# A state-space block with a gated feed-forward part on one core: two GpSimd chains of four operations per chunk become one chain over eight columns

## The reference

```python
x = x + attn(layernorm(x))     # attn: in_proj -> causal conv (4 taps) -> silu -> dt, B, C
                               # h[t] = exp(delta*A)*h[t-1] + delta*B*x  (16 states x 512 channels)
                               # y = sum_n h*C + D*x ; out_proj(y * silu(z))
x = x + ffn(layernorm(x))      # shared expert relu(x Ws1)^2 Ws2, plus top-2 of 8 experts weighted by
                               # trunc(softmax weight), which is 0 unless one weight is 1
```

## Time and profile before

| | us |
|---|---|
| median of 3 runs | 1577.25 (1576.58 to 1578.4) |
| the profiled execution's own time | 1574.1 |
| its span in the trace | 1572.0 |
| busy in the span: DVE, PE, POOL, ACT | 1474.5, 1443.9, 1411.7, 1258.6 |
| mean granted TensorE clock | 0.994 of full |

### The profile page before, as it was taken

One profiled execution on the slowest core, in us unless ns is written; L12 is line 12 of the kernel. 1 busy time (PEld: TensorE's weight loads), 2 busy tenths in 40 slices (PEclk: granted clock), 3 DMA queues, 4 the chain that ended last, 5 costly groups with the idle time before them and its releaser, 6 DMA issues.

```text
span 1572.0 us, 39373 instructions
## 1 busy us (share of the span) xinstructions
PE 1443.9 (92%) x15160; PEld 1119.7 (71%) x15160; DVE 1474.5 (94%) x1773; ACT 1258.6 (80%) x2100; POOL 1411.7 (90%) x1248
## 2 busy tenths in 40 slices
PE   8788999999999999999999999999999999998876
PEld 5666777776777777777776777777777677776765
DVE  6999999999999999999999999999999999998884
ACT  7887887887888888787888888788788888787651
POOL 2899998999999999998999999899998999899893
PEclk9999999999999999999999999999999999999998
DMA  5103031040402204031130402204031130402201
GB/s 154 65 3 135 2 105 60 13 152 3 153 12 69 95 3 162 2 122 42 22 143 3 162 1 77 89 3 162 3 131 33 42 110 3 149 1 86 79 15 42
DMA packets 78512, 106.46 MB, mean 68 GB/s; under 512 B 42289, under 2 KB 67761, under 8 KB 70130
## 3 DMA queue, kind: packets, MB, share of 16 engines
q1 hardware_dynamic: 78322, 103.92, 20.6%
HBM read 86.10 MB, written 17.30 MB: 66 GB/s over the span
## 4 chain that ended last, share of the span: by engine, by line
DVE 29%; ACT 19%; PE 19%; issue 16%; POOL 11%; DMA 2%; SPq 2%; DVEq 1%; ACTq 0%; POOLq 0%
DVE hs L941 26%; POOL hs L1229 9%; PE BX L236 8%; ACT da L605 8%; PE Y L296 3%; SPq L1358 2%; DMA cb<-c_scratch 2%; PE Y L260 2%; ACT xc L672 1%; PE PB L346 1%; ACT u L710 1%; ACT xp L640 1%; ACT x2n L742 1%; ACT u L708 1%; DVE Y L972 1%
## 5 line engine op out<-in xcount | busy, mean ns | idle before, releaser
L1229 POOL TENSOR_TENSOR hs<-hs,cb 128x1024 f32<-128x1024 f32 x512 | 1211.8, 2368 | 67.1 <-DVE hs L941 45.2
L941 DVE TENSOR_TENSOR_SCAN hs<-da,BX 128x512 f32<-128x512 f32 x1024 | 1165.5, 1201 | 61.0 <-PE BX L236 51.5
L605 ACT ACTIVATE da<-delta,a_neg 128x511 f32<-128x511 f32 (+1 forms) x1024 | 663.5, 711 | 25.1 <-DVE hs L941 24.8
L260 PEld LDWEIGHTS Y<-ident,hs 128*128 128x128 f32 x4096 | 464.4, 141 | 96.2 <-issue 61.5
L260 PE MATMUL Y<-ident,hs 128*128 128x128 f32 x4096 | 511.9, 273 | 11.1 <-POOL hs L1229 11.0
L236 PE MATMUL BX<-bd,uT 32*128 32x128 f32 x8192 | 302.7, 284 | 97.3 <-DVE hs L941 93.0
L236 PEld LDWEIGHTS BX<-bd,uT 32*128 32x128 f32 x8192 | 253.6, 187 | 157.9 <-DVE hs L941 155.4
L296 PE MATMUL Y<-xnT,w_in 128*128 128x512 f32 x240 | 118.1, 615 | 0.9 <-ACT xnT L621 0.9
L640 ACT ACTIVATE xp<-Y 128x512 f32<-128x512 f32 x60 | 35.9, 599 | 100.3 <-PE Y L296 99.7
L321 PE MATMUL PA<-w_in,xnT 128*128 128x512 f32 x240 | 114.5, 599 | 0.0
L972 DVE SCALAR_TENSOR_TENSOR Y<-xp,w_conv,Y 128x512 f32<-128x512 f32 x120 | 88.8, 740 | 2.3 <-ACT Y L642 0.7
(11 more groups left out here) (184 smaller groups left out, 1493.7 us busy)
## 6 DMA issues: line engine op xcount, KB each, us to landing
cb<-c_scratch SPq DMA_DIRECT2D x64, 1024.0 KB, 4.8
x<-in_x SPq DMA_DIRECT2D x16, 512.0 KB, 3.9
x_scratch<-x2T SPq DMA_DIRECT2D x16, 512.0 KB, 6.8
xt<-in_x SPq DMA_DIRECT2D x15, 512.0 KB, 4.9
bd<-bt SPq DMA_DIRECT2D x480, 1.0 KB
out<-x SPq DMA_DIRECT2D x15, 512.0 KB, 3.1
w_in<-in_in_wT SPq DMA_DIRECT2D x1, 1024.0 KB, 8.3
c_scratch<-dbc SPq DMA_DIRECT2D x64, 8.0 KB, 1.5
```

The lines of the kernel that those rows point to most:

```text
L260: mm = e.matmul(Y[(G * c + g) % 2][:, t * P:(t + 1) * P], hs[:, k % HR, q, t * P:(t + 1) * P], ident[:, :], is_transpose=True, start=False ...
L605: e.activation(da[:, k % DR, q, h:], delta[:, g, h:], ACT.Exp, scale=a_neg[:, g, n:n + 1]).then_inc(s_da, 1)
L941: e.tensor_tensor_scan(hs[:, k % HR, q, :], da[:, k % DR, q, :], BX[:, :].rearrange("p (t n) -> p n t", n=RT)[:, n % RT, :], float(c % HV) ...
L1229: e.tensor_tensor(hs[:, k % HR, :, :], hs[:, k % HR, :, :], cb[:, Q * p:Q * p + Q, :], ALU.mult).then_inc(s_hc, 1)
```

## The change

The chain of the second norm of chunk c - 1 and the chain of the input norm of chunk c + 3 become one chain over eight columns, at s == 21, for the chunks c = 1 to 12 of the loop (`BOTH`). The tiles `mv`, `ve`, `rstd`, `neg` and `shift` become eight columns wide; their first half serves the input norm, their second half the second norm. In these chunks the chain counts on the semaphores of the input norm, so those who wait for the second norm's result wait for `s_sh` (`shifted2`). It waits for both aggregations. In chunk 0 the input norm's chain, still four columns, moves from s == 25 to s == 21. In chunks 13 to 15 `pool_rstd2` stays as it was. The count waits of the last chunk are renumbered to fit.

```diff
@@ -96,19 +96,18 @@
-        mhalf = sb("mhalf", [P, TB])
-        minus = sb("minus", [P, TB])
-        epsv = sb("epsv", [P, TB])
+        mhalf = sb("mhalf", [P, 2 * TB])
+        minus = sb("minus", [P, 2 * TB])
+        epsv = sb("epsv", [P, 2 * TB])
...
-        mv = sb("mv", [P, TB, 2])
...
-        shift = sb("shift", [P, TB])
+
+        mv_b, ve_b, rstd_b, neg_b, shift_b = (sb("mv", [P, 2 * TB, 2]), sb("ve", [P, 2 * TB]), sb("rstd", [P, 2 * TB]),
+                                              sb("neg", [P, 2 * TB]), sb("shift", [P, 2 * TB]))
+        mv, ve, rstd, neg, shift = (mv_b[:, 0:TB, :], ve_b[:, 0:TB], rstd_b[:, 0:TB], neg_b[:, 0:TB], shift_b[:, 0:TB])
@@ -129,11 +128,8 @@
-        mv2 = sb("mv2", [P, TB, 2])
...
-        shift2 = sb("shift2", [P, TB])
+        mv2, ve2, rstd2, neg2, shift2 = (mv_b[:, TB:2 * TB, :], ve_b[:, TB:2 * TB], rstd_b[:, TB:2 * TB],
+                                         neg_b[:, TB:2 * TB], shift_b[:, TB:2 * TB])
@@ -170,6 +166,12 @@
+        BOTH = (1, NQ - 4)
+
+        def shifted2(c):
+            return (s_sh, c + 5) if c + 1 <= BOTH[1] else (s_sh2, c + 1 - BOTH[1])
@@ -732,7 +734,7 @@
         def act_norm2(e, c):
-            e.wait_ge(s_sh2, c + 1)
+            e.wait_ge(*shifted2(c))
@@ -996,7 +998,8 @@
         def dve_aggr2(e, c):
             e.wait_ge(s_st2, TB * (c + 1))
-            e.wait_ge(s_sh2, c)
+            if c:
+                e.wait_ge(*shifted2(c - 1))
@@ -1251,24 +1254,30 @@
         def pool_rstd(e, c):
             e.wait_ge(s_mv, TB * (c + 1))
             e.wait_ge(s_xn, c)
-            e.tensor_tensor(ve[:, :], mv[:, :, 1], epsv[:, :], ALU.add).then_inc(s_ve, 1)
-            e.tensor_tensor(neg[:, :], mv[:, :, 0], minus[:, :], ALU.mult).then_inc(s_neg, 1)
+            n = TB
+            if BOTH[0] <= c - 3 <= BOTH[1]:
+                n = 2 * TB
+                e.wait_ge(s_mv2, TB * (c - 3))
+                e.wait_ge(s_xn2, c - 4)
+            e.tensor_tensor(ve_b[:, 0:n], mv_b[:, 0:n, 1], epsv[:, 0:n], ALU.add).then_inc(s_ve, 1)
+            e.tensor_tensor(neg_b[:, 0:n], mv_b[:, 0:n, 0], minus[:, 0:n], ALU.mult).then_inc(s_neg, 1)
             e.wait_ge(s_ve, c + 1)
-            e.tensor_tensor(rstd[:, :], ve[:, :], mhalf[:, :], ALU.pow).then_inc(s_rs, 1)
+            e.tensor_tensor(rstd_b[:, 0:n], ve_b[:, 0:n], mhalf[:, 0:n], ALU.pow).then_inc(s_rs, 1)
             e.wait_ge(s_neg, c + 1)
             e.wait_ge(s_rs, c + 1)
-            e.tensor_tensor(shift[:, :], neg[:, :], rstd[:, :], ALU.mult).then_inc(s_sh, 1)
+            e.tensor_tensor(shift_b[:, 0:n], neg_b[:, 0:n], rstd_b[:, 0:n], ALU.mult).then_inc(s_sh, 1)
@@ -1309,11 +1318,11 @@
-                    if s == 21 and on(c - 1):
+                    if s == 21 and c > BOTH[1]:
                         pool_rstd2(e, c - 1)
                     if s == 30 and on(c - 1):
                         pool_gap(e, c - 1)
-                    if s == 25 and on(c + 3):
+                    if s == 21 and on(c + 3):
                         pool_rstd(e, c + 3)
```

More of the change, by code:

```diff
@@ L106, in mamba_moe @@
         st = sb("st", [P, TB, 6])
-        mv = sb("mv", [P, TB, 2])
-        ve = sb("ve", [P, TB])
-        rstd = sb("rstd", [P, TB])
-        neg = sb("neg", [P, TB])
-        shift = sb("shift", [P, TB])
+        mv_b, ve_b, rstd_b, neg_b, shift_b = (sb("mv", [P, 2 * TB, 2]), sb("ve", [P, 2 * TB]), sb("rstd", [P, 2 * TB]),
+                                              sb("neg", [P, 2 * TB]), sb("shift", [P, 2 * TB]))
+        mv, ve, rstd, neg, shift = (mv_b[:, 0:TB, :], ve_b[:, 0:TB], rstd_b[:, 0:TB], neg_b[:, 0:TB], shift_b[:, 0:TB])
         xnT = [sb(f"xnT{i}", [P, KD, CH]) for i in range(2)]
@@ L131, in mamba_moe @@
         st2 = sb("st2", [P, TB, 6])
-        mv2 = sb("mv2", [P, TB, 2])
-        ve2 = sb("ve2", [P, TB])
-        rstd2 = sb("rstd2", [P, TB])
-        neg2 = sb("neg2", [P, TB])
-        shift2 = sb("shift2", [P, TB])
+        mv2, ve2, rstd2, neg2, shift2 = (mv_b[:, TB:2 * TB, :], ve_b[:, TB:2 * TB], rstd_b[:, TB:2 * TB],
+                                         neg_b[:, TB:2 * TB], shift_b[:, TB:2 * TB])
         x2n = sb("x2n", [P, TB, DM])
@@ L907, in scalar @@
             for h in range(2):
-                e.wait_ge(s_sh2, NQ + h)
+                e.wait_ge(s_sh2, NQ - BOTH[1] + h)
                 for t in (2 * h, 2 * h + 1):
@@ L1193, in vector @@
                 e.wait_ge(s_st2, TB * (NQ - 1) + 2 * (h + 1))
-                e.wait_ge(s_sh2, NQ - 1)
+                e.wait_ge(*shifted2(NQ - 2))
                 for t in (2 * h, 2 * h + 1):
@@ L1264, in pool_rstd2 @@
             e.wait_ge(s_xn2, c)
[L1265 to L1271, removed]
+            n = c + 1 - BOTH[1]
+            e.tensor_tensor(ve2, mv2[:, :, 1], epsv[:, 0:TB], ALU.add).then_inc(s_ve2, 1)
+            e.tensor_tensor(neg2, mv2[:, :, 0], minus[:, 0:TB], ALU.mult).then_inc(s_neg2, 1)
+            e.wait_ge(s_ve2, n)
+            e.tensor_tensor(rstd2, ve2, mhalf[:, 0:TB], ALU.pow).then_inc(s_rs2, 1)
+            e.wait_ge(s_neg2, n)
+            e.wait_ge(s_rs2, n)
+            e.tensor_tensor(shift2, neg2, rstd2, ALU.mult).then_inc(s_sh2, 1)
         def pool_gap(e, c):
@@ L1325, in gpsimd @@
                 e.tensor_tensor(neg2[:, part], mv2[:, part, 0], minus[:, part], ALU.mult).then_inc(s_neg2, 1)
-                e.wait_ge(s_ve2, NQ + h)
+                e.wait_ge(s_ve2, NQ - BOTH[1] + h)
                 e.tensor_tensor(rstd2[:, part], ve2[:, part], mhalf[:, part], ALU.pow).then_inc(s_rs2, 1)
-                e.wait_ge(s_neg2, NQ + h)
-                e.wait_ge(s_rs2, NQ + h)
+                e.wait_ge(s_neg2, NQ - BOTH[1] + h)
+                e.wait_ge(s_rs2, NQ - BOTH[1] + h)
                 e.tensor_tensor(shift2[:, part], neg2[:, part], rstd2[:, part], ALU.mult).then_inc(s_sh2, 1)
```

## The result

| | before | after |
|---|---|---|
| median, timed side by side, 20 runs each, us | 1575.96 (1572.54 to 1581.81) | 1572.35 (1568.34 to 1579.87) |
| ratio, 95% interval | | 0.9978 (0.9969 to 0.9987) |
| the same, in a second session of 11 runs and 29 of before | 1575.99 | 1573.14, ratio 0.9982 (0.9973 to 0.9991) |
| profiled execution, its span | 1574.1, 1572.0 | 1571.58, 1569.8 |

The change makes the kernel faster by 0.2%. The profiled execution is close to what the sum said (1571.5, and a span of 1569.4). That it comes so close is luck: a second profiled execution of the same kernel took 1568.82. The two hardly differ up to the first scan of chunk 15 (1445.66 and 1445.67 us from the start), and from there to the end, where TensorE's clock fell at other places in each, it is 124.1 us in the first, 121.4 in the second and 124.3 before.

A forecast was written before the change was run, and what follows sets the result against it. The prediction took a DVE and PE ring with a 5.85 us beat as the bound. 3.5 us won less 0.9 lost gave 2.6 off the 1577.25 median: 1574.6, range 1572.6 to 1578.4.

The forecast's parts named there:

- the sum: Whole kernel: 3.5 us won less 0.9 lost, 2.6 us off, for a profiled execution of 1571.5 and span of 1569.4.
- The bound: DVE and PE form a ring, four scans and the refill of `BX`, 5.85 us per pair of steps; POOL matters only where late.
- The price of the power: POOL's chain at step 21: power costs 156 ns a column, 1638 ns for eight, so the chain grows 0.63 us.
- The rival by which the price is one per instruction: POOL's chain does not grow with eight columns, nothing is lost at step 26, all 3.5 us come: 1573.7; chance 0.1.
- Step 30: Even chunks 2 to 12: POOL's product of step 27 comes earlier, beat falls from 6.37 to 5.85, 0.52 us won six times.
- The rival with PE's own order in its place: PE's order at step 29 holds step 30 in even chunks; only 0.34 won against 0.9 lost: 1577.8; chance 0.12.
- Step 26: Even chunks: the longer merged chain makes `BX` 0.08 to 0.21 us late, taken as 0.15 six times, 0.9 us lost; odd chunks nothing.
- The rest, at nothing: ACT's second norm, the wait for both aggregations, step 25's u, DMA and wider constants were all said to cost nothing.
- Chunk 0: Moving its four-column chain from step 25 to 21 returns 0.34 us at step 30, where the beat was 6.19.
- The slower case: POOL's power at eight columns costs more than 156 ns a column; break-even at growth 1.0 us, 1585.7 at 1.5; chance 0.06.
- a clock stretch: A stretch of lower TensorE clock, one more or less, moves any case by 0.7 to 1.4 us; no case of its own.
- the case without a loss at step 26: The chain keeps its length, POOL is 1.6 us earlier, and all 3.5 us come: 1573.7; chance 0.1.

The follow-up runs named there:

- the longer chain: The changed kernel with one more two-column power in each of the twelve merged chains, written to an unread tile: 1575.76 us, ratio 0.9996 to before.

## Why the prediction was wrong in its number and right in its steps

- **The bound.** Right: the beat of 5.85 us is in all ten traces, and POOL's 10.4 us less work became 2.1 us in chunks 1 to 14.
- **The price of the power.** Right: 1642 ns for 1638. The rival by which the price is one per instruction is out. The rule of the Trainium skill (GPSIMD Engine Reference, section 3.1), some 2.6 cycles an element, fits the add (207 ns at eight columns, 198 at four) and not the power, which takes 157 ns a column.
- **Step 30.** Right: 6.37 became 5.85 in six chunks. The rival with PE's own order in its place is out.
- **Step 26.** Right in place and kind, 0.18 for an assumed 0.15, within the bounds of 0.08 to 0.21. The odd chunks paid nothing. The slack before was 0.65 - 0.18 = 0.47 in the even chunks (0.42 to 0.55 worked out) and, by the longer chain, 0.65 + 0.39 = 1.04 in the odd ones (0.95 worked out).
- **The rest, at nothing.** Right but for one row: ACT's second copy of the transposes now waits 0.17 us for PE, and no beat shows it. The second norm starts behind ACT's exponentials as before, with the chain already done.
- **Chunk 0.** Right: 0.34 at step 30. The profiled execution did not show it in its time because the clock took 0.85 in the same chunk.
- **The slower case.** Not met. Its working gave break-even at a growth of the chain of 1.0 us. By the measured slacks, 6 x (g - 0.47) + 6 x (g - 1.04) = 3.5 is met at g = 1.05 (the second term barely begins there). One part of it was wrong: I let the gain at step 30 shrink as the chain grows. At the longer chain's growth of 0.65 + 0.49 = 1.14 that would leave step 30 late by 0.06, and it is 5.85, since DVE itself is later by then.
- **The number.** The step that failed is the end of the sum, "for the median I say 1577.25 - 2.6", and the range hung on it. 1577.25 was the median of three runs. Over 20 runs it is 1575.96, and single runs reach from 1572.54 to 1581.81. The range had room for a clock stretch on either side of the forecast and none for the median before being 1.3 us off. From 1575.96 the same 2.6 us give 1573.4. Set on 1575.96, the range would have been 1571.3 to 1577.1 and held the result. The remaining 1.0 is inside the interval of the ratio (2.0 to 4.9 us), and no beat shows it. The steps are confirmed by the beats, 2.44 us for 2.6; the timed gain alone, with that interval, could not tell 2.6 from the 3.5 of the case without a loss at step 26.

## What to carry to other kernels

Find the beat of the ring that paces the kernel, and look for the beats that are too long; an engine at 90% that does not lengthen one of them has nothing to give. For work on such an engine, tell apart taking it away from moving it: moved work delays the next place that is near its limit, and an in-order engine's slack is found by subtracting, at each such place, what stands between the late input and the next link of the ring. When the gain is smaller than the spread between runs, count the beats in the trace and take the base time from many runs.

## What the runs showed of the hardware

TensorE's granted clock falls at different places in executions of the same kernel. In the first trace of the change it is 0.66 on average from 112 to 117 us, in the second it is 1.00 there, 0.86 from 64 to 76 us and 0.76 from 117 to 124 us; the profiled execution of before has 1.00 in all three. In chunk 0 around 108 to 127 us this cost 0.85 us in the first (one beat of 6.70) and 0.57 + 0.35 = 0.92 us in the second (6.42 and 6.20). From 123 to 1421 us it is 1.00 in all ten traces, and there the beats that no edit touches repeat within 0.06 us. The time from the first scan of chunk 15 to the end varies from 121.4 to 126.7 us, by more than the change is worth. Over the 20 runs of the change the longest span, 1578.1, has the lowest mean clock, 0.985, and the nine runs at 0.992 and above lie between 1566.6 and 1570.7. So much of the spread between single runs, 9.3 us before and 11.5 after, goes with the clock.

And an added GpSimd power of 0.69 us in the middle of a chain lengthened the chain by 0.49 only, since the operation behind it had started 0.14 us after the one ahead ended, and the added one filled that pause.
